# One windowed-attention stack on one Trainium2 core: attention output transposed in 32x32 blocks by VectorE, head sums halved on GpSimd, inverse roots by Ln and Exp, and reordered stages

## What is computed

```
def attn_layer(x, Wqkv, qs, ksc, Wo):            # 16 heads of 64, inner width 1024
    q, k, v = split heads of x @ Wqkv
    q = l2norm(q) * qs ;  k = l2norm(k) * ksc    # l2norm: t / max(|t|, 1e-12), per token and head
    q = q*cos*scale + rotate_half(q)*sin*scale   # k with 1/scale
    out = local_attention(q, k, v)               # windows of 32 tokens, keys of this window and the one before
    return out @ Wo
def ffn_layer(x, g, bln, W1, b1, W2, b2):
    xn = (x - mu) / sqrt(var + 1e-05) * g + bln
    a, gate = split(xn @ W1 + b1)
    return a * gelu(gate) @ W2 + b2
for i in range(6):
    x = attn_layer(shift_tokens(x), ...) + x
    x = ffn_layer(shift_tokens(x), ...) + x
```

## Time and profile before

| | us |
|---|---|
| median of 3 runs | 4425.67 |
| lowest and highest of them | 4416.88, 4430.52 |
| the profiled execution, its whole time | 4425.53 |
| its span, first to last instruction | 4423.6 |

### The profile page before, as it was taken

The page is one execution under the profiler, slowest core; times in us unless marked ns, Lnnn a source line. Parts: engine busy times, 40 slices in busy tenths (PEclk is TensorE's granted clock), DMA queues, the critical chain, the costliest instruction groups (busy, mean ns, idle before and its releaser), DMA issues. The chain is left out here.

```text
span 4423.6 us, 152875 instructions
## 1 busy us (share of the span) xinstructions
PE 3800.6 (86%) x62881; PEld 2217.6 (50%) x63136; DVE 3733.5 (84%) x5604; ACT 2440.2 (55%) x2858; POOL 1736.7 (39%) x3224
## 2 busy tenths in 40 slices
PE   5888885898988899988988889998889898898996
PEld 2333333555555555555555555555455555555554
DVE  7888886898987989878888879888888888788885
ACT  3666663555555555555555555555555555555653
POOL 2222223444443444434444434444444444344441
PEclk8999998999999999999999999999999999999998
DMA  0000002010111111010101111010101011110102
GB/s 25 1 1 1 1 1 72 24 35 21 39 35 38 31 29 31 29 54 21 35 25 34 40 38 31 25 34 24 54 26 31 28 29 45 33 35 21 38 22 57
DMA packets 59405, 131.83 MB, mean 30 GB/s; under 512 B 9540, under 2 KB 31432, under 8 KB 58824
## 3 DMA queue, kind: packets, MB, share of 16 engines
q1 hardware_dynamic: 58824, 122.45, 9.5%
HBM read 21.99 MB, written 4.19 MB: 6 GB/s over the span
## 5 line engine op out<-in xcount | busy, mean ns | idle before, releaser
L731 POOL TENSOR_TENSOR cosq<-cosq,sinq 128x1024 f32<-128x1024 f32 x384 | 950.2, 2474 | 1588.5 <-DVE sinq L781 1588.5
L1009 PE MATMUL slot<-w_qkv,xs 128*128 128x512 f32 x2304 | 1109.3, 611 | 49.4 <-ACT xs L870 19.6
L1009 PEld LDWEIGHTS slot<-w_qkv,xs 128*128 128x128 f32 x2304 | 412.9, 194 | 454.7 <-issue 378.1
L816 DVE TENSOR_TENSOR qk<-cosq,ry 128x1024 f32<-128x1024 f32 x384 | 559.0, 1475 | 94.0 <-POOL ry L723 48.7
L882 ACT ACTIVATE sq<-slot 128x1024 f32<-128x1024 f32 x384 | 393.4, 1024 | 212.9 <-PE slot L1009 211.7
L781 DVE TENSOR_TENSOR sinq<-slot,table 128x512 f32<-128x512 f32 x768 | 490.5, 680 | 0.0
L778 DVE TENSOR_TENSOR cosq<-slot,table 128x1024 f32<-128x1024 f32 x384 | 467.8, 1218 | 24.4 <-ACT sq L882 13.2
L962 PE MATMUL slot<-ident,qk 128*128 128x128 f32 x3072 | 410.3, 277 | 69.9 <-issue 63.3
L962 PEld LDWEIGHTS slot<-ident,qk 128*128 128x128 f32 x3072 | 355.5, 142 | 208.8 <-issue 197.4
L800 DVE TENSOR_REDUCE ss<-sq 128x32 f32<-128x2048 f32 x192 | 437.2, 2277 | 10.3 <-ACT sq L882 10.1
L910 ACT ACTIVATE prob<-prob 128x1024 f32<-128x1024 f32 x192 | 203.1, 1058 | 375.7 <-DVE prob L825 374.0
(11 more groups left out here) (127 smaller groups left out, 6193.0 us busy)
## 6 DMA issues: line engine op xcount, KB each, us to landing
vb<-va SPq DMA_DIRECT2D x192, 390.0 KB, 3.5
vb<-va SPq DMA_DIRECT2D x144, 130.0 KB, 3.6
w_qkv<-in_w_qkv SPq DMA_DIRECT2D x18, 512.0 KB, 4.5
w_o<-in_w_o SPq DMA_DIRECT2D x6, 512.0 KB
w<-in_w SPq DMA_DIRECT2D x6, 342.0 KB
res<-in_x SPq DMA_DIRECT2D x4, 512.0 KB, 6.2
kept<-res SPq DMA_DIRECT2D x1, 2048.0 KB, 8.7
out<-fin_res SPq DMA_DIRECT2D x8, 256.0 KB, 2.4
```

Source lines behind the costliest of these rows:

```text
L731: nc.gpsimd.tensor_tensor(cosq[:, side], cosq[:, side], sinq[:, side], ALU.add).then_inc(S["qk"[side] + "_added"], 1)
L816: nc.vector.tensor_tensor(qk[:, side], cosq[:, side].rearrange("p h a d -> p h (a d)"), ry[:, side * HEADS:(side + 1) * HEADS, None].broad ...
L1009: last = nc.tensor.matmul(slot(kind, n)[:, i, :], xs[:, n * P:(n + 1) * P], w_qkv[:, "qkv".index(kind), i * SEQ:(i + 1) * SEQ], start=True ...
```

## The change

In `windowed_stack`:

- **Output transpose.** The PE stage `o` (8 transposes of 128x128 per tile) and its ACT copy are gone. A new DVE stage `turn` transposes `o` in blocks of 32x32, one instruction of 128x1024 per tile, straight into `oT`. The rows of `w_o` are reordered to match on the host, and its DMA moves whole rows.
- **Inverse norms.** A new POOL stage `fold` adds the two halves of the squares (an add of 128x1024 per tile). DVE then sums 32 instead of 64 features and takes the maximum with 1e-24. The Newton steps are gone; a new ACT stage `norm` does Ln and then Exp with scale -0.5 on 128x32.
- **Rotation.** The two products with `sin` of 128x512 become one of 128x1024 that reads the halves in reversed order.
- **Second half.** The mean and the subtraction become one product with the identity minus 1/128 (`centre`). Variance: Ln and Exp on ACT in place of Sqrt there and the reciprocal on DVE. The affine step moves from DVE to ACT (`affine`). One table of ACT now holds Ln and Exp; it changes to Gelu and back once in a unit.
- **Weight waits.** The waits at the end of a layer's first turn are gone; PE waits in `wo`, ACT in `affine`, DVE in `hid`, in the turns after.
- **Orders and slots.** All five tables and `SLOTS_OF` are new.

```
 PE_ORDER = stages(
-    "o0- r1- s2- q0 kT3- va1- k0 vb1- qT3- r2- o1- s3- va2- vb2- q1 r3- k1 o2- qT0 va3- vb3- kT0 k2 o3- s0 wo- q2 "
-    "v0 mean- qT1 r0 var- v1 kT1 k3 va0 s1 h0- h1- h2- vb0 q3 v2 qT2 y- kT2 v3 ")
+    "k0 q0 qT3- r2- kT3- vb2- va2- s3- q1 k1 r3- qT0 kT0 v0 va3- q2 vb3- k2 s0 wo- qT1 kT1 r0 v1 centre- s1 var- "
+    "k3 v2 q3 va0 kT2 h0- h1- qT2 vb0 h2- r1 s2 v3 y- va1 vb1 ")
 DVE_ORDER: now  "turn1- rotate_k0 rotate_q0 vb2- norms0 va2- s3- scale_q0 scale_k0 rotate_q1 turn2- rotate_k1 ..."
 ACT_ORDER: now  "next- v3- square_k0 exp2- square_q0 qT3- r2- kT3- norm0 exp3- square_q1 r3- qT0 ..."
 POOL_ORDER = stages(
-    "add_k3- root3- add_q3- add_q0 root0 add_k0 add_q1 root1 add_k1 add_q2 root2 add_k2 ")
+    "fold0 add_k0 add_q0 add_q1 fold1 add_k1 fold2 add_q2 add_k2 fold3 add_q3 add_k3 ")
 SP_ORDER = stages(
-    "vb2- vb3- vb0 vb1 ")
+    "vb0 vb1 vb2 vb3 ")
...
+                if kind == "fold":
+                    for name in "qk":
+                        wait(pool, name + "_squared", unit, t)
+                    wait_tile(pool, "sumsq", unit, t)
+                    squares = sq[:, :, :, :].rearrange("p a h (e d) -> p (a h) e d", e=2)
+                    nc.gpsimd.tensor_tensor(half_sq[:, :, :], squares[:, :, 0, :], squares[:, :, 1, :],
+                                            ALU.add).then_inc(S["folded"], 1)
...
+                elif kind == "turn":
+                    for name in ("va", "vb"):
+                        wait(dve, name + "_read", unit, n)
+                    wait(dve, "wo_filled", unit - 1)
+                    nc.vector.transpose(oT[:, n, :, :, :, :, :].rearrange("p a w r e t -> p (a w r e t)"),
+                                        o[:, :, :, :, :].rearrange("p a w r d -> p (a w r d)")).then_inc(S["turned"], 1)
...
+                elif kind == "norm":
+                    wait(act, "sumsq", unit, n)
+                    nc.scalar.activation(logs[:, :], ss[:, :], ACT.Ln).then_inc(S["log_link"], 1)
+                    act.wait_ge(S["log_link"], unit * TPB + n + 1)
+                    for name in "qk":
+                        wait_tile(act, name + "_scaled", unit, n)
+                    nc.scalar.activation(ry[:, :], logs[:, :], ACT.Exp, scale=-0.5).then_inc(S["rooted"], 1)
...
+        def wait_ff(eng, starts, layer):
+            if starts is None and layer is not None:
+                eng.wait_ge(S["w_ff"], 16 * W_FF * (layer + 1))
```

## The result

| | before | after |
|---|---|---|
| median, us | 4427.8 | 4458.5 |
| lowest and highest, us | 4416.9, 4430.5 | 4454.6, 4459.1 |
| span of the profiled execution, us | 4423.6 | 4457.0 |
| mean granted clock of TensorE | 0.972 | 0.942 |

The medians are of four runs each; the ratio is 1.0072, 95% interval 1.0054 to 1.0091. (Of all executions behind this document one, of b_all, ran in a slower state, 5093 us at a granted clock of 0.735; it is left out.) The prediction was 4136 us with a range of 4050 to 4280 and 0.93 on faster. **It was wrong**, by 323 us.

What follows compares the result with a forecast made beforehand. The prediction took PE's own stream, work plus its own stalls, to bound the 75.0 us turn. From 4425.5 us, -254 for 47 turns at 69.6, -30 where layers begin and -6 for first and last turn gave 4136, range 4050 to 4280.

Steps and rivals of the forecast that it cites:

- PE's idle time after: PE's idle time in a turn of the changed kernel: 5.8 us, between 3.9 and 8.5, down from 7.4.
- one of 0.8 at the branch: Stall of PE at the loop's branch, taken as 0.8 us of the 4.2 us of stalls left in a turn.
- Two of 1.7: Two PE stalls of 1.7 us each in a turn, in the long runs of small products that remain.
- PE's work, 63.8 us: PE's work in a turn falls from 67.6 to 63.8 us as the output transpose, 3.8 us, leaves PE.
- The wait ahead of `r3`: New PE wait before transpose `r3` for tile 3's maximum, subtraction and Exp: 1.6 us, between 0.3 and 2.5.
- No stall stands between `va3` and `vb3`: On PE, `q2` now stands between these two stages of small products, so no stall was expected there.
- rival 4: GpSimd's adds and VectorE's scalings block each other, up to 2.1 us a meeting; turn 77 us, total 4484 us; chance 0.04.
- a fourth of 0.6 us: On DVE, of 0.6 us behind each sum over heads, one operation in four stays; four times -0.45, -1.8 us a unit.
- Where a layer begins: At five layer starts the extra time falls from 12.8 to 6.8 us, `k0` waiting 4.8 for its weights; -30 us in all.
- Rival 1: PE's idle time doesn't shrink, stalls follow the count of small products, `r3` adds its wait; turn 72.8, total 4286 us; chance 0.15.
- I'm wrong if 'issue' stays at 6: Sign against the forecast: PE's idle time ending with "issue", 6.2 us a unit before, stays at 6.

Runs made afterwards that it cites:

- b_all: The kernel before with all parts of the change, but in its own orders and slots, only adapted to the new stages: 4735.2 us, ratio 1.071.
- b_edge: The kernel before with the loop's edge moved on PE alone, so that `o0 r1 s2` stand last in a turn instead of first: 4659.0 us, ratio 1.053.
- a_unroll: The changed kernel with the inner loops over the sequences written out, same order of work: 4129.0 us, ratio 0.933.
- a_best: The changed kernel with the loops over the sequences written out and SP's `vb3` copies started later, behind `r2` of the next turn: 4125.0 us, ratio 0.931.
- a_best_nomax: a_best without the maximum with 1e-24 on DVE; Ln adds 1e-24 as its bias instead: 4084.1 us, ratio 0.921.
- a_nomax: The changed kernel, still looped, without the maximum on DVE; Ln takes a bias instead: 4416.6 us, ratio 0.996.
- b_late: The kernel before with only the late waits for the second half's weights: 4484.0 us, ratio 1.014.
- b_unroll: The kernel before with the inner loops over the sequences written out, order of work unchanged: 4459.8 us, ratio 1.009.
- a_pad: The changed kernel with 128 semaphore instructions on PE, executed once ahead of the stack's loops, shifting all later PE code: 4356.3 us, ratio 0.982.

## Why the prediction was wrong

**The step that failed is "PE's idle time after".** It counted "one of 0.8 at the branch". That number was about right for the kernel before (0.9 on average), where `y`, `kT2` and `v3` stand ahead of the jump, and it was carried over to a stream with `va1 vb1` there: 64 tiny products in some 1.6 us. The text had even named them, "`va1 vb1` at the loop's end", without asking what covers the jump now. Measured: 6.05 us of idle time in the turn shown (5.5 on average), and 2.9 more in `k0 q0` through the clock. The branch itself takes 5.44 us in the median (4.07 before), so the forecast had the remainder of a covered jump in place of a bare one. b_edge shows the same in the kernel before, and the seams without a jump show its absence.

The Trainium skill (Runtime: NRT & Kernel Launch, Instruction fetch mechanics) states that fetching ahead is sequential and that a taken branch to a target outside the current two blocks has to fetch it before execution goes on. The trace agrees: one or two packets of instructions start within each taken jump of PE's loop over the sequences, and the idle time is 5 to 6 us behind tiny products in the later layers, 2.4 with `y` between, 0.5 to 1.7 behind 5 us of large ones. The prediction cited the section for its blocks and passed over this sentence.

**A stall within the small runs: right in kind, too small.** Two of 1.7 were taken. a_unroll has one of 1.33 and sometimes a second; the looped kernel has 2.74 + 1.47 in one run of small products, 1.49 with the code shifted. As each of the two opens (at 1842.75 and 1847.25), a packet of instructions is under way or just landing, from 1842.27 to 1843.64 and from 1846.36 to 1847.32. That fits a fetch that falls behind, but packets run elsewhere without a stall, and no run tests it. The prediction counted 64 products and their loads as half a block of 256; the trace has 128 records of products and 128 of loads in a stage of scores, which fill one.

**PE's work, 63.8 us: right.** a_unroll measures 63.77. The wait ahead of `r3`, forecast at 1.6, is 0.8 in a_unroll (27.4 us, 36 times) and absent in most turns of the looped kernel, where the stall in `s3` covers it. No stall stands between `va3` and `vb3`, as forecast. With two small waits not forecast (1.1 for `hid`, 0.4 to 0.65 for `probT`), the idle time without the jump is 4.2 us in the turn shown and about 5.1 on average, and 5.8 was taken.

**DVE, ACT, POOL: mostly right.** Rows of the view of groups by form, of the kernel after (compare; columns: busy us, mean ns, idle before), and one of the query on L796 (minimum, median, maximum in ns):

```profile
L829 DVE STREAM_TRANSPOSE oT<-o 128x1024 f32<-128x1024 f32 x192 | 237.4, 1236 | 0.3
L795 DVE TENSOR_REDUCE ss<-half_sq 128x32 f32<-128x1024 f32 x192 | 231.9, 1208 | 1.8 <-POOL half_sq L728 1.7
L804 DVE TENSOR_TENSOR qk<-cosq,ry 128x1024 f32<-128x1024 f32 x384 | 457.8, 1213 | 32.4 <-ACT ry L922 30.1 <-POOL cosq L733 2.3
```

```profile
L796 DVE TENSOR_SCALAR ss<-ss x192: 180/1316/2069, 709.8 to 4373.5; 128x32 f32<-128x32 f32 x192
```

The transpose was forecast at 1.25 us and takes 1.24, the sum at 1.216 and 1.208. The scalings keep 1213 ns, so rival 4 didn't come at the place it named. It came at one that the prediction priced at 0.15, a fourth of 0.6 us: the maximum, 1316 ns in the median. The timelines of POOL and DVE show one such meeting; L796 starts within POOL's two adds and ends with them:

```profile
2068.12 4.67 POOL L733 TENSOR_TENSOR cosq<-cosq,sinq 128x1024 f32<-128x1024 f32 x2
...
2070.92 1.91 DVE L796 TENSOR_SCALAR ss<-ss 128x32 f32<-128x32 f32 x1
```

Four of these are 4.6 us a turn above their undisturbed 180 ns, but DVE's total missed by 2.3 only, so other terms were set too high. Its cost to the kernel is 41 us, by a_best against a_best_nomax, and 42 by after against a_nomax: not what made the change slower. The prediction took from the Trainium skill that an operation with one SBUF input doesn't contend. The same section (SBUF, State Buffer; Who interferes with whom) excepts what enters a two-port mode and names `tensor_scalar`; the trace agrees with the exception, here and in b_late.

**Where a layer begins.** A pair of turns there was forecast at 2 x 69.6 + 6.8 = 146.0 us and takes 149.0 (162.9 before). The mechanism was right: nobody waits for the weights of the second half, and `k0` waits for its own. SP's timeline with the issue of the load, and PE's with the wait for it:

```profile
1904.35 0.36 SPq L684 DMA_DIRECT2D w_qkv<-in_w_qkv  x1
...
1911.87 5.46 PE L1002 MATMUL slot<-w_qkv,xs 128*128 128x512 f32 x8 [7.69 <-DMA w_qkv<-in_w_qkv]
```

7.69 us for 4.8 forecast: the loads land after 5.9 us in the median (4.5 before), and they run through the same time as the jump, which ordinary turns pay in full. Against turns without a jump (a_unroll: pairs 150.3, turns 68.9) a layer's begin costs 12.5 us, and 6.8 was forecast.

**The rivals.** Rival 1 (idle time doesn't shrink, 4286) was the nearest in kind, but it too took the stalls as given and had no term for the jump. No rival had a stall of PE's own grow. Rival 4's 4484 lies nearest to the measured 4458.5, but by luck: its mechanism, scalings that GpSimd blocks, didn't come. The slower side held only 0.04 of the chance, and all of it stood on GpSimd.

**What the text named as signs.** "I'm wrong if 'issue' stays at 6": it is at (198.6 + 84.2 + 64.9) / 48 = 7.2 us a unit, and at 10.3 in the turn shown. The sign was right, and it wasn't turned into a rival with a price.

**What stays open.** Why ordinary turns of later layers, not those of the first, rose in b_late; why b_unroll's turns didn't become shorter; how PE's stalls depend on the position of the code, beyond the one shift of a_pad and the count of packets; and how much each part of the change is worth alone, since b_all had orders of its own.

## What to carry to other kernels

Where a loop's order is changed, look first at what each engine does in the last microseconds ahead of the jump: here some 5 us of large, slow instructions covered most of it, tiny ones uncovered it, and behind the 6 us of idle time TensorE's granted clock was 0.54. The branch has rows of its own in the trace, with its duration; read them ahead of any forecast, in the kernel before too. Write the loop out, or move its seam, before a new order is judged: with the loops written out the changed kernel is 7.4% faster than the old one (4129.0 for 4459.8 us), and looped it is 0.7% slower. And look for the seam that has no jump in the same trace (a first turn, a turn outside the loop); it is a control at no cost.

## What was not expected of the hardware

- A taken jump of PE lasted 3.4 to 6.0 us in the kernel after, with one or two packets of 16 KB on the instruction queue, and one of DVE 56 ns; behind 64 tiny products it left PE idle for 6.05 us, and the granted clock of the following 6.4 us was 0.54.
- 128 instructions that run once, ahead of the loops, made the kernel 102 us (2.3%) faster and swapped slow and fast turns between the two copies of the loop.
- The same edit, loops written out, took 7.4% off one order and added 0.9% to the other.
- A VectorE operation on 32 elements a partition, 180 ns alone, took 1316 ns in the median beside GpSimd's adds, and one of 545 ns took 2657. The 128x1024 sums, transposes and scalings in the same turns took at most 1.2% more than their medians (1219, 1247 and 1227 ns at the most).
